# Row work, statistics and weight loads in other slots, and the spreads of the inverted denominators issued from ScalarE

## The chip, the cores and the metric

The kernel runs on one core of one Trainium2 chip. The metric is the device time of one execution in microseconds (us), as the median of several runs. All times below are microseconds unless marked otherwise. The engines are PE (TensorE, matmuls), DVE (VectorE), ACT (ScalarE), POOL (GpSimd) and SP (SyncE, which here only issues DMAs). Each engine works through a queue of its own in order, and waits on semaphores for the others.

## The reference

One transformer block in float32 over 16 sequences of 256 rows and 256 columns: self attention, cross attention to a context of 192 columns, and a gated feed-forward part (FFN).

```python
def _attention(xq, xkv, wq, wk, wv, wo, bo):
    q = (xq @ wq).reshape(B, S, N_HEADS, D_HEAD)
    k = (xkv @ wk).reshape(B, T, N_HEADS, D_HEAD)
    v = (xkv @ wv).reshape(B, T, N_HEADS, D_HEAD)
    attn = jnp.einsum('bihd,bjhd->bhij', q, k) * D_HEAD ** (-0.5)
    attn = jax.nn.softmax(attn, axis=-1)
    out = jnp.einsum('bhij,bjhd->bihd', attn, v).reshape(B, S, D_ATTN)
    return out @ wo + bo
h = _layernorm(x, ln1_g, ln1_b)
x = _attention(h, h, sa_wq, sa_wk, sa_wv, sa_wo, sa_bo) + x
h = _layernorm(x, ln2_g, ln2_b)
x = _attention(h, cond_emb, ca_wq, ca_wk, ca_wv, ca_wo, ca_bo) + x
h = _layernorm(x, ln3_g, ln3_b)
p = h @ ff_w1 + ff_b1
a, gate = (p[..., :D_FF], p[..., D_FF:])
h = a * jax.nn.gelu(gate, approximate=False) @ ff_w2 + ff_b2
return h + x
```

There are 16 heads of 64, so 8 pairs of heads, and D_FF is 1024.

## The kernel before

**Slots.** The work of the two attentions is cut into ATT = 256 slots, one for each pair of heads of each sequence, first all of self attention (slots 0 to 127), then all of cross attention (128 to 255). n counts the 32 pairs of a sequence and an attention; n from 16 on are the cross ones. Slot c is named by its scores. Each engine has a function that writes its part of slot c (pe_slot, act_slot, dve_slot, pool_slot, and on SP a loop in the block at L1549), and the order of the statements in it is the order in the engine's queue. Nothing is scheduled by a planner. After the slots comes the FFN: NCK = 8 chunks of two sequences, 8 steps each. gates(c) and second(c) are PE's two products of step c; the first steps are laced into the last slots by hand (L1849 on).

**One slot.** PE computes the scores S of slot c from RX (the split Q and K in a ring, brought there by SP's DMAs from QKS), projections QKB of a later pair, values VB, the output product WOP of an earlier slot, the transposes PTB of the exponentials of slot c-1, and the product with the values PVB of slot c-2. DVE takes the maximum of the scores (NM, L945), ACT the exponential with its sum (PT, DEN, L780). DVE inverts the sums (RDEN, L985) and turns them (RDT, L987). ACT copies the transposed exponentials to PH (L813), DVE makes their low part PL (L889). Both parts of QKB go to QKS: ACT's copy is the high part, DVE's split (L903) the low part. Every float32 matrix is multiplied as such a high and a low part.

**Denominators.** SP saves RDT to DRAM (save_den, L1605) and brings it back over 64 partitions for each of the two heads (spread_den, two DMAs into RB, L1616). ACT copies half of PVB into ON (L756), DVE adds the other half (L965), POOL multiplies ON by RB (L1143). Its count is pl_or.

**Row work.** The rows of a sequence are normalised some slots before it starts: start_of(n) = 8n - 20 from n = 6 on. Relative to that slot DVE takes the statistics at -4 (dve_stats), aggregates at -3, and POOL makes the reciprocal root at -3; DVE normalises at -1 (dve_normalize, L850) into the buffer near(n); SP stores the rows at 0, ACT loads them turned at +1 (L681), DVE turns them at +2, ACT applies gain and bias at +3 and +4 (L664), and POOL splits them after that. The context rows of cross attention are loaded by ACT at -5 to -3 (L699). Every fourth slot, c = 3 modulo 4, DVE adds four finished slots of WOP to the residual XR (L915, L919).

**Rows of the FFN.** chunk 0 and chunk 1 are prepared within the last slots. In dve_attention_slot their statistics (L831) and normalisations (L850) stand behind all of dve_slot, that is at the slot's end: chunk 0 at c = FFN_START - 16 to - 9 (FFN_START = ATT - 10 = 246), chunk 1's statistics at ATT - 6 to ATT - 4 and its normalisation in step 3 of the FFN. ACT rounds chunk 1 (L1325, L1330) in step 6, act_copy_raw (L1253) copies first products aside (RAW) while QKB is still shared with the attention.

## Time and profile before

| what | us |
|---|---|
| median of 3 runs (lowest to highest) | 1696.74 (1695.99 to 1697.89) |
| the profiled execution, whole | 1697.57 |
| its span, first to last instruction | 1695.8 |
| PE busy | 1680.5 (99%) |
| DVE busy | 1396.4 (82%) |
| ACT busy | 1247.5 (74%) |
| POOL busy | 1079.5 (64%) |

The profiled execution is 0.83 above the median of the runs. The granted clock of TensorE is 1.000 over the whole span. Busy time is arithmetic only: issuing a DMA occupies an engine's queue and is listed apart, as ACTq or SPq. In a timeline a line gives start and duration of a group of equal instructions (x4 is four of them), and in brackets the idle time ahead of the first and what ended it. A matmul's end is modelled: the next one of a pipelined row starts before it.

### The profile page before, as it was taken

The page shows a single profiled execution, that of the slowest core. Times are in us where ns is not written, and L with a number is a line of the kernel's source. Part 1 is how long each engine was busy: PE and PEld are TensorE (multiplying, and loading weights), DVE is VectorE, ACT ScalarE, POOL GpSimd, SP SyncE. Part 2 cuts the span into 40 slices and gives each one's busy share as a digit, 9 for nine tenths or more (in the row PEclk, how much of TensorE's full clock was granted, in tenths as well). Part 3 has the DMA queues.
Part 4 walks back from the last instruction along what each step waited for, and adds up shares of the span by engine and source line. Part 5 has one row for each costly group of instructions (what it writes and reads, how often), then busy time and mean ns, then how long its engine had stood idle before and what let it go on. Part 6 is the DMA issues. An engine that isn't in the chain of part 4 may idle for free.

```text
span 1695.8 us, 39063 instructions
## 1 busy us (share of the span) xinstructions
PE 1680.5 (99%) x11712; PEld 1560.7 (92%) x11712; DVE 1396.4 (82%) x2964; ACT 1247.5 (74%) x3379; POOL 1079.5 (64%) x1804
## 2 busy tenths in 40 slices
PE   8999999999999999999999999999999999999999
PEld 8999999999999999999999999999999998888888
DVE  8887888888888888889888888888888877656665
ACT  7788788888888888888888888888888886122221
POOL 7776577777766666787777777777777565231211
PEclk9999999999999999999999999999999999999999
DMA  7776677778766567887787878787776785212110
GB/s 214 183 180 161 171 208 190 204 198 211 196 176 159 153 167 200 230 222 185 190 209 196 205 196 210 193 210 182 197 177 176 192 211 139 69 50 72 64 40 26
DMA packets 301138, 288.91 MB, mean 170 GB/s; under 512 B 103425, under 2 KB 252033, under 8 KB 300929
## 3 DMA queue, kind: packets, MB, share of 16 engines
q1 hardware_dynamic: 247136, 273.29, 61.8%
q10 hardware_dynamic: 53792, 13.12, 3.5%
q8 instruction: 96, 1.57, 0.4%
q14 instruction: 114, 0.93, 0.2%
HBM read 82.98 MB, written 37.49 MB: 71 GB/s over the span
## 4 chain that ended last, share of the span: by engine, by line
PE 89%; DVE 3%; SPq 3%; issue 2%; POOL 1%; DMA 1%; ACT 1%; ACTq 0%; DVEq 0%; POOLq 0%
PE QKB L556 16%; PE PVB L638 13%; PE PTB L569 11%; PE WOP L620 10%; PE VB L491 8%; PE S L458 6%; PE S L459 6%; PE S L1282 5%; PE PTB L1282 5%; PE QKB L1304 3%; PE VB L1304 3%; PE QKB L538 2%; SPq L673 1%; SPq L675 1%; SPq L1616 1%
## 5 line engine op out<-in xcount | busy, mean ns | idle before, releaser
L780 ACT ACTIVATE PT<-S,NM 128x256 f32<-128x256 f32 x1024 | 471.9, 473 | 147.2 <-DVE NM L945 146.0
L889 DVE TENSOR_TENSOR PL<-PTB,PH 128x512 fp32r<-128x512 f32 x512 | 350.9, 686 | 128.2 <-ACT PH L813 127.9
L1143 POOL TENSOR_TENSOR ON<-ON,RB 128x256 f32<-128x256 f32 x256 | 188.1, 735 | 287.4 <-DVE ON L965 265.5
L945 DVE TENSOR_REDUCE NM<-S 128x2 f32<-128x512 f32 x512 | 327.3, 681 | 0.3
L813 ACT ACTIVATE PH<-PTB 128x1024 fp32r<-128x1024 f32 x256 | 264.3, 1032 | 67.9 <-PE PTB L569 66.3
L569 PE MATMUL PTB<-IDN,PT 128*128 128x128 f32 x2048 | 265.7, 273 | 0.1
L458 PE MATMUL S<-RX 128*128 128x256 f32 x1012 | 253.9, 283 | 0.8 <-DMA RX<-QKS 0.8
L459 PE MATMUL S<-RX 128*128 128x256 f32 x1012 | 253.7, 283 | 0.0
L556 PE MATMUL QKB<-HT,WQ 128*128 128x512 f32 x936 | 242.9, 394 | 0.9
L620 PEld LDWEIGHTS WOP<-WO,OT 128*128 128x128 f32 x1536 | 217.5, 190 | 20.1 <-POOL OT L1148 0.2
L569 PEld LDWEIGHTS PTB<-IDN,PT 128*128 128x128 f32 x2048 | 229.5, 140 | 1.1 <-issue 0.5
L620 PE MATMUL WOP<-WO,OT 128*128 128x256 f32 x1536 | 224.3, 282 | 0.0
L965 DVE TENSOR_TENSOR ON<-PVB,ON 64x256 f32<-64x256 f32 x512 | 213.4, 417 | 3.6
L756 ACT ACTIVATE ON<-PVB 64x256 f32<-64x256 f32 x512 | 194.2, 379 | 22.5 <-issue 5.0
L780 ACT ACTIVATION_READ_ACCUMULATOR PT<-S,NM 128x1 f32 x1024 | 207.7, 203 | 0.0
L1148 POOL TENSOR_TENSOR OT<-ON,OT 128x256 fp32r<-128x256 f32 x256 | 189.9, 742 | 20.5
L1124 POOL TENSOR_TENSOR VR<-VF,VR 128x256 fp32r<-128x256 f32 x256 | 189.1, 739 | 20.5
L458 PEld LDWEIGHTS S<-RX 128*128 128x128 f32 x1012 | 193.4, 191 | 1.2 <-DMA RX<-QKS 1.2
L459 PEld LDWEIGHTS S<-RX 128*128 128x128 f32 x1012 | 194.3, 192 | 0.0
L556 PEld LDWEIGHTS QKB<-HT,WQ 128*128 128x128 f32 x936 | 165.7, 189 | 30.4 <-DVE QKS L903 3.2
L638 PE MATMUL PVB<-PH,VR 128*128 128x256 f32 x1024 | 183.4, 300 | 0.7 <-issue 0.6
L638 PE MATMUL PVB<-PL,VR 128*128 128x256 f32 x1024 | 163.4, 282 | 0.0
(163 smaller groups left out, 2918.7 us busy)
## 6 DMA issues: line engine op xcount, KB each, us to landing
RX<-QKS SPq DMA_DIRECT2D x506, 192.0 KB, 2.9
RX<-QKS SPq DMA_DIRECT2D x506, 128.0 KB, 2.8
RB<-denominators SPq DMA_DIRECT2D x512, 64.0 KB, 2.7
out_dram<-XR SPq DMA_DIRECT2D x32, 256.0 KB, 3.5
weights_qk<-SPL SPq DMA_DIRECT2D x32, 256.0 KB, 3.4
WQ<-weights_qk SPq DMA_DIRECT2D x32, 256.0 KB, 3.4
rows<-XN SPq DMA_DIRECT2D x24, 256.0 KB, 2.6
rows<-HF SPq DMA_DIRECT2D x23, 256.0 KB, 2.7
```

The source lines that it names most:

```text
L458: e.matmul(o, q, RX[:, c % 2, i, K1, :], start=True, stop=False)
L459: last = e.matmul(o, q, RX[:, c % 2, i, K2, :], start=False, stop=True)
L556: last = e.matmul(QKB[:, :], w_pair(w, wp, p), act, start=i == 0, stop=i == len(passes) - 1)
L569: last = e.transpose(PTB[:, i, kt * S + qt * P:kt * S + (qt + 1) * P], PT[:, s % 2, q0:q0 + P], IDN[:, :])
L620: last = e.matmul(WOP[:, t * D:(t + 1) * D], OT[:, op, t * P:(t + 1) * P], WO[:, p, wp, :], start=begins(s) and t == 0 and j == 0, stop=en ...
L638: last = e.matmul(PVB[:, i * S:(i + 1) * S], VR[:, s // 2 % 2, kt, s % 2, i * P:(i + 1) * P], part[:, first:first + S], start=i == 0 and j ...
L756: last = e.activation(ON[OWN[i], s % 2, :], PVB[OTHER[i], i * S:(i + 1) * S], ACT.Copy)
L780: last = e.activation(PT[:, c % 2, j * S:(j + 1) * S], S1[:, i, qt * S:(qt + 1) * S], ACT.Exp, bias=NM[:, j:j + 1], accum_out=DEN[:, c % 2 ...
L813: e.activation(PH[:, s % 2, :], PTB[:, :, :].rearrange("p i n -> p (i n)"), ACT.Copy) \
L889: e.tensor_tensor(PL[:, cols], PTB[:, i, :], PH[:, s % 2, cols].bitcast(F32), ALU.subtract).then_inc(a.dve_pl, 1)
L945: e.tensor_reduce(NM[:, i * TT:(i + 1) * TT], S1[:, i, :].rearrange("p (t s) -> p t s", t=TT), AX.X, ALU.max, negate=True).then_inc(a.dve_ ...
L965: last = e.tensor_tensor(on, PVB[OWN[i], i * S:(i + 1) * S], on, ALU.add)
```

## The change

Lines of the changed kernel lie some 9 to 56 further on than the same lines before.

1. **normalized_in.** For n = 6 to 15 the normalisation moves from start_of(n) - 1 to start_of(n) - 2. The others stay.
2. **First value copies.** The copies VF of slots 0 to 7 wait for pl_v >= v - 3 instead of v.
3. **Spreads.** spread_den moves from SP to ACT's queue, behind the copies ON of the slot, with the same two waits.
4. **dve_ffn_rows.** The statistics and normalisations of FFN chunks 0 and 1 move into the slot, behind the other row work and ahead of the reciprocal. For chunk 1 the statistics go to ATT - 12 to - 10, the reciprocal root on POOL to ATT - 9, the normalisation to ATT - 7 to - 4, one tile per slot. SP stores those rows at ATT - 5 and - 3; act_copy_raw(4) and (5) wait for these stores, and the loads of these rows for their halves on DVE. In the FFN the turns of chunk 1 are made in steps 3 and 4 (5 and 6 before), and ACT rounds it in step 4 (6 before).
5. **Loads on SP.** The third and fourth quarters' chunks, load_four and the load of BOUT are issued in other slots.
6. **PE.** gates(5) goes before second(1).

```diff
@@ -154,6 +154,15 @@
+def normalized_in(c):
+    n = due(c, -2, 2)
+    if n and OLD // PAIRS + 2 <= n < B:
+        return n
+    n = due(c, -1, 2)
+    return None if n and OLD // PAIRS + 2 <= n < B else n
...
@@ -742,6 +751,18 @@
+        def spread_den(e, s):
+            e.wait_ge(d_ds[s % 4], 16 * (s // 4 + 1))
+            if s >= 2:
+                e.wait_ge(a.pl_or, s - 1)
+            else:
+                e.wait_ge(s_ow, s + 1)
+            for i in range(2):
+                e.dma_start(RB[OWN[i], s % 2, :],
+                            DS[s % 4, TT * i:TT * (i + 1), :].rearrange("t p -> (t p)").partition_broadcast(P // 2)) \
+                    .then_inc(d_rb[s % 2], 16)
...
@@ -755,6 +776,9 @@
                     last = e.activation(ON[OWN[i], s % 2, :], PVB[OTHER[i], i * S:(i + 1) * S], ACT.Copy)
                 last.then_inc(a.act_lp, 1)
+            if 0 <= c - 2 < ATT:
+                spread_den(e, c - 2)
             if due(c, 1, 2):
                 act_load_rows(e, due(c, 1), 0, 1)
...
@@ -925,14 +949,43 @@
-            if due(c, -1, 2):
-                e.wait_ge(a.dve_th, due(c, -1) - 1)
-                dve_normalize(e, sl, a, due(c, -1), (near(due(c, -1)),))
+            n = normalized_in(c)
+            if n:
+                e.wait_ge(a.dve_th, n - 1)
+                dve_normalize(e, sl, a, n, (near(n),))
...
+        def dve_ffn_rows(e, c):
...
+            if c == ATT - 12:
+                e.wait_ge(a.dve_xo, B + HOLD + 4)
+                dve_stats(e, zero_ffn, fs, 1, 0, 1)
+            if c == ATT - 11:
+                dve_stats(e, zero_ffn, fs, 1, 2, 3)
+            if c == ATT - 10:
+                dve_aggregate(e, zero_ffn, fs, 1)
+            if c == ATT - 7:
+                e.wait_ge(fs.s_ht, KD)
+            if ATT - 7 <= c < ATT - 3:
+                dve_normalize(e, zero_ffn, fs, 1, ROWS, (c - ATT + 7,))
...
@@ -968,7 +1021,7 @@
-                sl.wait(e, a.pl_v, v)
+                sl.wait(e, a.pl_v, v - 3)
...
             dve_rows(e, sl)
+            dve_ffn_rows(e, c)
...
@@ -1253,6 +1307,8 @@
             e.wait_ge(fs.pe_raw, n + 1)
+            if n in (4, 5):
+                e.wait_ge(d_fs[n - 4], 16 * 2)
...
@@ -1312,6 +1368,8 @@
                 e.wait_ge(d_fs[h], 16 * (chunk + 1))
+                if chunk == 1:
+                    e.wait_ge(fs.dve_hf, 2)
...
@@ -1352,7 +1410,7 @@
-            if c >= 0 and c % PAIRS == 6 and sl.has(c + PAIRS):
+            if c >= 0 and c % PAIRS == (6 if c >= PAIRS else 4) and sl.has(c + PAIRS):
...
@@ -1434,10 +1492,10 @@
-                if f == (2 if chunk else 3):
+                if f == 2 and chunk:
                     sl.wait(e, fs.s_ht, KD * (chunk + 1))
                     dve_normalize(e, sl, fs, chunk + 1, ROWS)
-                turn = f - (4 if chunk else 5)
+                turn = f - (4 if chunk else 3)
...
@@ -1684,12 +1709,14 @@
+                            turns = ((0, 1, 2, 3), (0, 1, 3, 4))[quarter - 2]
...
-                            if c == at + chunk:
+                            if c == at + turns[chunk]:
...
-                            if c == four + 2 + 2 * n:
+                            if c == four + 2 + (n if g == 0 else 3 * n):
...
@@ -1745,19 +1772,19 @@
-                if c == ATT - PAIRS:
+                if c == ATT - 19:
                     e.wait_ge(a.pl_xb, 2 * B)
                     e.dma_start(BOUT[:, :], ff_b2.partition_broadcast(P)).then_inc(d_bo, 16)
             for c in range(-AHEAD, ATT + 2):
-                if c >= 2:
-                    spread_den(c - 2)
...
+                if c in (ATT - 5, ATT - 3):
+                    store_ffn_rows(1, (c - ATT + 5) // 2)
...
@@ -1862,8 +1890,8 @@
             pe_outputs(e, ATT - 3)
+            pe_gates(e, EARLY + 1)
             pe_second(e, 1)
-            pe_gates(e, EARLY + 1)
             pe_outputs(e, ATT - 2)
```

DVE in slots 66 and 67 of self attention, before the change, from the sum of slot 66's two ON halves (L965) to the turn of slot 67's denominators. L903 is the split, L919 the residual sum, L850 the normalisation of n = 11.

```order
L965 TENSOR_TENSOR ON<-PVB,ON 64x256 x2
L985 RECIPROCAL RDEN<-DEN 128x4
L987 STREAM_TRANSPOSE RDT<-RDEN 128x32
L903 TENSOR_TENSOR QKS<-QKB,QKS 128x2x256
L889 TENSOR_TENSOR PL<-PTB,PH 128x512
L945 TENSOR_REDUCE NM<-S 128x2 x2
L889 TENSOR_TENSOR PL<-PTB,PH 128x512
L965 TENSOR_TENSOR ON<-PVB,ON 64x256 x2
L919 TENSOR_TENSOR XR<-WOP,XR 128x512
L850 TENSOR_SCALAR XN<-XR,MV,RSTD 128x2x4x32 x2
L985 RECIPROCAL RDEN<-DEN 128x4
L987 STREAM_TRANSPOSE RDT<-RDEN 128x32
```

The same stretch after the change.

```order
L1018 TENSOR_TENSOR ON<-PVB,ON 64x256 x2
L874 TENSOR_SCALAR XN<-XR,MV,RSTD 128x2x4x32 x2
L1039 RECIPROCAL RDEN<-DEN 128x4
L1041 STREAM_TRANSPOSE RDT<-RDEN 128x32
L927 TENSOR_TENSOR QKS<-QKB,QKS 128x2x256
L913 TENSOR_TENSOR PL<-PTB,PH 128x512
L998 TENSOR_REDUCE NM<-S 128x2 x2
L913 TENSOR_TENSOR PL<-PTB,PH 128x512
L1018 TENSOR_TENSOR ON<-PVB,ON 64x256 x2
L943 TENSOR_TENSOR XR<-WOP,XR 128x512
L1039 RECIPROCAL RDEN<-DEN 128x4
L1041 STREAM_TRANSPOSE RDT<-RDEN 128x32
```

The two normalisations have gone from slot 67, which has the residual sum, to slot 66, ahead of the reciprocal and the split there.

ACT in slot 144 of cross attention before, from the copies ON to the exponentials. L664 is a gain and bias, L699 a load of context rows.

```order
L756 ACTIVATE ON<-PVB 64x256 [waits pl_o,pe_pv]
L756 ACTIVATE ON<-PVB 64x256
L664 ACTIVATE HF<-HF,LNG 128x256 [waits dve_th]
L699 DMA XN<-in_ctx_dram 32x8x32 [waits dve_th]
L780 ACTIVATE PT,DEN<-S,NM 128x256 [waits dve_nm,dve_rc,pe_t]
L780 ACTIVATE PT,DEN<-S,NM 128x256
L780 ACTIVATE PT,DEN<-S,NM 128x256 [waits dve_nm]
L780 ACTIVATE PT,DEN<-S,NM 128x256
```

The same place after the change.

```order
L777 ACTIVATE ON<-PVB 64x256 [waits pl_o,pe_pv]
L777 ACTIVATE ON<-PVB 64x256
L762 DMA RB<-denominators 64x256 [waits pl_or,d_ds2]
L762 DMA RB<-denominators 64x256
L673 ACTIVATE HF<-HF,LNG 128x256 [waits dve_th]
L708 DMA XN<-in_ctx_dram 32x8x32 [waits dve_th]
L804 ACTIVATE PT,DEN<-S,NM 128x256 [waits dve_nm,dve_rc,pe_t]
L804 ACTIVATE PT,DEN<-S,NM 128x256
L804 ACTIVATE PT,DEN<-S,NM 128x256 [waits dve_nm]
L804 ACTIVATE PT,DEN<-S,NM 128x256
```

The two DMAs into RB now stand behind the copies ON and ahead of the gain and bias and the four exponentials, and they wait for a multiplication on POOL (pl_or) and for the save of the denominators (d_ds2).

PE at the entry of the FFN before, from the output product of slot ATT - 3. L1304 is the second product, L1282 the gates.

```order
L620 MATMUL WOP<-WO,OT 128x256 x6
L1304 MATMUL QKB<-WV,QKS 128x256 x6
L1304 MATMUL VB<-WV,QKS 128x256 x6
L1282 MATMUL PTB<-HT,WQ 128x512 x12
L620 MATMUL WOP<-WO,OT 128x256 x6
L1304 MATMUL QKB<-WV,QKS 128x256 x6
L1304 MATMUL VB<-WV,QKS 128x256 x6
L620 MATMUL WOP<-WO,OT 128x256 x6
```

The same place after the change.

```order
L629 MATMUL WOP<-WO,OT 128x256 x6
L1338 MATMUL PTB<-HT,WQ 128x512 x12
L1360 MATMUL QKB<-WV,QKS 128x256 x6
L1360 MATMUL VB<-WV,QKS 128x256 x6
L629 MATMUL WOP<-WO,OT 128x256 x6
L1360 MATMUL QKB<-WV,QKS 128x256 x6
L1360 MATMUL VB<-WV,QKS 128x256 x6
L629 MATMUL WOP<-WO,OT 128x256 x6
```

The twelve matmuls of gates(5) now stand ahead of the second product of step 1; everything around is as before.

## Rows read from the trace of the kernel before

**Rows 1.** Page, part 1: engine, busy us, share of the span, instructions.
```profile
PE 1680.5 (99%) x11712; PEld 1560.7 (92%) x11712; DVE 1396.4 (82%) x2964; ACT 1247.5 (74%) x3379; POOL 1079.5 (64%) x1804
```
**Rows 2.** Waits of PE's weight loads: waiter, releaser: us in all, count, longest.
```profile
PEld QKB L556 <- DVE QKS L903: 3.2, 11, 0.3
...
PEld PVB L638 <- issue: 2.3, 8, 0.4
```
**Rows 3.** Timeline (start, us, engine, line, operation), PE in three slots of self attention.
```profile
395.33 0.28 PE L458 MATMUL S<-RX 128*128 128x256 f32 x1
...
396.29 1.55 PE L556 MATMUL QKB<-HT,WQ 128*128 128x512 f32 x6
...
400.89 0.28 PE L458 MATMUL S<-RX 128*128 128x256 f32 x1
...
406.80 0.28 PE L458 MATMUL S<-RX 128*128 128x256 f32 x1
```
**Rows 4.** Timeline, DVE in the same slots.
```profile
393.94 0.69 DVE L903 TENSOR_TENSOR QKS<-QKB,QKS 128x512 fp32r<-128x512 f32 x1
...
395.64 0.69 DVE L889 TENSOR_TENSOR PL<-PTB,PH 128x512 fp32r<-128x512 f32 x1 [1.01 <-ACT PH L813]
...
399.87 1.25 DVE L850 TENSOR_SCALAR XN<-XR,MV,RSTD 128x256 f32<-128x256 f32 x2
...
401.38 0.65 DVE L903 TENSOR_TENSOR QKS<-QKB,QKS 128x512 fp32r<-128x512 f32 x1
```
**Rows 5.** Timeline, DVE near the start.
```profile
18.33 0.42 DVE L972 COPY VF<-VB 128x256 f32<-128x256 f32 x1 [0.69 <-POOL VR L1124]
```
**Rows 6.** Timeline, PE: first scores of two slots of cross attention, twelve slots apart.
```profile
1285.72 0.28 PE L458 MATMUL S<-RX 128*128 128x256 f32 x1
...
1351.55 0.28 PE L458 MATMUL S<-RX 128*128 128x256 f32 x1
```
**Rows 7.** Timeline, SP and PE before slot 251.
```profile
1391.02 0.62 SPq L675 DMA_DIRECT2D RX<-QKS  x1
...
1392.61 1.10 SPq L1616 DMA_DIRECT2D RB<-denominators  x2
...
1396.07 0.39 PE L458 MATMUL S<-RX 128*128 128x256 f32 x1 [0.79 <-DMA RX<-QKS]
```
**Rows 8.** Timeline, ACT and its DMA issues (ACTq), self and cross attention.
```profile
501.34 1.94 ACTq L681 DMA_DIRECT2D HF<-rows  x2
...
811.32 0.77 ACT L756 ACTIVATE ON<-PVB 64x256 f32<-64x256 f32 x2
...
812.73 0.48 ACT L780 ACTIVATE PT<-S,NM 128x256 f32<-128x256 f32 x1 [0.65 <-DVE NM L945]
...
816.55 0.32 ACTq L699 DMA_DIRECT2D XN<-in_ctx_dram  x1
...
816.65 0.77 ACT L756 ACTIVATE ON<-PVB 64x256 f32<-64x256 f32 x2
```
**Rows 9.** Timeline, ACT, DVE and PE around a slot with gain and bias.
```profile
822.94 0.60 ACT L664 ACTIVATE HF<-HF,LNG 128x256 f32<-128x256 f32 x1
...
829.73 0.85 DVE L965 TENSOR_TENSOR ON<-PVB,ON 64x256 f32<-64x256 f32 x2
...
831.32 0.72 PE L638 MATMUL PVB<-PH,VR 128*128 128x256 f32 x4
```
**Rows 10.** Timeline, PE and ACT at the entry of the FFN.
```profile
1433.94 0.98 PE L1304 MATMUL QKB<-WV,QKS 128*128 128x256 f32 x6 [0.60 <-DVE QKS L1418]
...
1443.05 1.20 PE L1282 MATMUL S<-HT,WQ 128*128 128x512 f32 x4 [1.57 <-DVE PT L1412]
...
1451.98 0.81 ACT L1325 ACTIVATE PH<-XN,LNG 128x512 fp32r<-128x512 f32 x1 [5.19 <-DVE HF L1364]
...
1454.81 0.67 ACT L1353 ACTIVATE PT<-PTB,B 128x512 f32<-128x512 f32 x1
...
1456.37 1.88 PE L1282 MATMUL S<-PH,WQ 128*128 128x512 f32 x7 [1.82 <-POOL PH L1383]
```

More of the change, by code:

```diff
@@ L935, in dve_rows @@
                 dve_aggregate(e, sl, a, due(c, -3))
+        def dve_ffn_rows(e, c):
+            if c == FFN_START - 16:
+                e.wait_ge(a.dve_xo, B + HOLD + 2)
+                dve_stats(e, zero_ffn, fs, 0, 0, 1)
+            if c == FFN_START - 15:
+                dve_stats(e, zero_ffn, fs, 0, 2, 3)
+            if c == FFN_START - 14:
+                dve_aggregate(e, zero_ffn, fs, 0)
+            if c == FFN_START - 12:
+                e.wait_ge(a.s_ht, 4 * B)
+                e.wait_ge(a.pl_ct, 2 * B)
+            if FFN_START - 12 <= c < FFN_START - 8:
+                dve_normalize(e, zero_ffn, fs, 0, ROWS, (c - FFN_START + 12,))
+            if FFN_START - 6 <= c < FFN_START - 4:
+                dve_ffn_turn(e, 0, c - FFN_START + 6)
+            if c == ATT - 12:
[9 more added lines that the diff above has]
+                dve_normalize(e, zero_ffn, fs, 1, ROWS, (c - ATT + 7,))
         def dve_slot(e, sl):
@@ L1496, in dve_attention_slot @@
                 dve_aggregate(e, sl, a, 1)
-            if c == FFN_START - 16:
-                e.wait_ge(a.dve_xo, B + HOLD + 2)
-                dve_stats(e, zero_ffn, fs, 0, 0, 1)
-            if c == FFN_START - 15:
-                dve_stats(e, zero_ffn, fs, 0, 2, 3)
-            if c == FFN_START - 14:
-                dve_aggregate(e, zero_ffn, fs, 0)
-            if c == ATT - 6:
-                e.wait_ge(a.dve_xo, B + HOLD + 4)
-                dve_stats(e, zero_ffn, fs, 1, 0, 1)
-            if c == ATT - 5:
-                dve_stats(e, zero_ffn, fs, 1, 2, 3)
-            if c == ATT - 4:
-                dve_aggregate(e, zero_ffn, fs, 1)
-            if c == FFN_START - 12:
-                e.wait_ge(a.s_ht, 4 * B)
-                e.wait_ge(a.pl_ct, 2 * B)
-            if FFN_START - 12 <= c < FFN_START - 8:
-                dve_normalize(e, zero_ffn, fs, 0, ROWS, (c - FFN_START + 12,))
-            if FFN_START - 6 <= c < FFN_START - 4:
-                dve_ffn_turn(e, 0, c - FFN_START + 6)
         def pool_low(e, *ns):
@@ L1538, in pool_attention_slot @@
                 pool_ffn_low(e, 1)
-            if sl.c == ATT - 3:
+            if sl.c == ATT - 9:
+                e.wait_ge(fs.dve_xn, 2)
                 pool_rstd(e, zero_ffn, fs, 1)
@@ L1606, in save_den @@
                             RDT[:, s % 2, :]).then_inc(d_ds[s % 4], 16)
-            def spread_den(s):
-                e.wait_ge(d_ds[s % 4], 16 * (s // 4 + 1))
-                if s >= 2:
-                    e.wait_ge(a.pl_or, s - 1)
-                else:
-                    e.wait_ge(s_ow, s + 1)
-                for i in range(2):
-                    e.dma_start(RB[OWN[i], s % 2, :],
-                                DS[s % 4, TT * i:TT * (i + 1), :].rearrange("t p -> (t p)").partition_broadcast(P // 2)) \
-                        .then_inc(d_rb[s % 2], 16)
             def stage_cross(n):
@@ L1690, in fill_weights @@
                             at = j - LEAD + 2
+                            turns = (0, 1, 2, 3)
                         for chunk in range(4):
-                            if c == at + chunk:
+                            if c == at + turns[chunk]:
                                 if chunk == 0:
@@ L1774, in _ @@
                 if chunk + 1 < NCK:
-                    store_ffn_rows(chunk + 1, 0, 1)
+                    if chunk:
+                        store_ffn_rows(chunk + 1, 0, 1)
                     load_ffn_rows(e, chunk + 1, *range(8))
```

## The prediction

> **What bounds the kernel now.** I read the engine totals first [rows 1]: PE is busy 1680.5 of 1695.8 us, 99%. No edit here removes a matmul, so all that can be won is what PE still waits, and all that can be lost is a new wait. The list of PE's waits comes next [rows 2]: the largest kind is the weight load of the joint projections (QKB) on the split of Q and K on DVE, 3.2 us in 11 waits, and the first product with V (PVB) waits 2.3 us in 8 places for its semaphores. The timeline then tells what the list hides. A matmul row is drawn 0.28 long, but the next one starts 0.12 later, so a wait under about 0.16 shows as no idle time; starts of slots have to be set against each other. The slots of self attention start at 395.33, 400.89 and 406.80 [rows 3]: 5.56, then 5.91. The reader is to see that one slot in eight is 0.35 too long, without an idle mark. The clock was at its full level in every slice, so I leave it out.
>
> **Part A, the normalisation of sequences 7 to 15.** In the slot of 5.91 DVE does two normalisations at 399.87 (1.25) right before the split at 401.38, behind which QKB starts [rows 3, 4]; in that same slot stands the residual sum of 0.7. The change takes the 1.25 out of it and puts it a slot earlier. There the split ended at 393.94 + 0.69 = 394.63, and QKB started at 396.29 [rows 3, 4]: 1.66 of slack against 1.25, so 0.41 is left; and the next DVE operation, PL at 395.64, had been idle 1.01, so it starts at most 0.24 later, which PV two thirds of a slot on does not feel. The wait goes, and nothing is late next. This holds for n = 7 to 15, nine slots: 9 x 0.35 = **3.2**. Sequences from 16 on are not moved, since the range ends at the 16 of self attention. If only half of the moved work fitted, it would be 1.6.
>
> **Part B, the first value copies.** DVE's copy VF at 18.33 had stood idle 0.69 behind the multiplication VR on POOL [rows 5]. Waiting for a product three slots older ends that; next in line would be PE's product VB itself. I take **0.6**, between 0 (something else of the start comes last) and 0.7.
>
> **Part C, row work in front of the split and earlier.** From the scores at 1285.72 to those at 1351.55 lie 12 slots of cross attention [rows 6]: 65.83, against 12 x 5.33 = 63.96, 1.9 over. (5.33 is the distance of ON copies in a quiet place, 811.32 to 816.65 [rows 8].) In these slots DVE does the statistics, normalisation and turns of the first FFN rows at the slot's end, behind the split, where they delay the maximum (NM) of the next scores. The same operations now stand ahead of the reciprocals. Where a slot holds 5.9 of DVE work for 5.33, which happens in two, no order helps. I take 1.4. Likewise the last twelve slots hold the second chunk's statistics at the slot's end; three of the eight PVB waits lie there [rows 2]. These statistics go to ATT-12 to -10, its normalisation to ATT-7 to -4, one tile each. I take 0.8. Together **2.2**, between 1.0 and 2.7. New is that the raw copies 4 and 5 on ACT wait for the stores of these rows. Those are issued at ATT-5 and -3, the copies stand at ATT-3 and -2. Even with the 5.05 from issue to use of the RX in [rows 7] a store lands within one slot, so the second is just in time. Behind a waiting raw copy stand the copy PH and so PV. I price it at nothing, at most 1.
>
> **Part D, the spreads leave SyncE.** Each slot two DMAs bring the inverted denominators back over 64 partitions each. On SP the pair takes 1.10 [rows 7]. Late in the attentions SP is full: RX is issued at 1391.02, and the scores that read it start at 1396.07 after 0.79 idle (0.96 by starts) [rows 7]. Without 1.1 per slot ahead of it, and with one load of weights gone to a slot eleven earlier, RX is issued about that much sooner. I count 1.0 here and 0.3 for a smaller wait of the same kind five slots before: **1.3**, between 0 and 1.6. What speaks against it: of the 5.05 from issue to use most is the transfer, which an earlier place in a queue doesn't shorten. The Trainium skill ("DMA: Bandwidth & Descriptors", section "Issuing engines are not separate DMA queues") says that starting DMAs from several engines saves only the sequencer's time to start them, usually small next to the DMA. Here the rows bear it out in part: the time to start a pair, 1.10, is a fifth of the 5.05, and by the strict rule part D would be 0 and the sum 1.3 less.
>
> **What the spreads cost on ACT.** The trace shows no such pair on ACT. Nearest rows [rows 8]: single issues on ACT of 0.32 (twice 0.64, the low end), the SP pair of 1.10 [rows 7], and a pair on ACT of 1.94 (the high end, at 501.34). I take 1.10, since it is the same transfer with the same descriptors. ACT's queue starts an issue before the arithmetic ahead of it has ended: 816.55 against 816.65 for the copy ON [rows 8]. So the pair lies from -0.1 to 1.0 behind the first ON copy, whose two parts end at 0.77, while Exp starts at 812.73 - 811.32 = 1.41, idle 0.65 on NM [rows 8]. Up to 1.45 a pair costs nothing. Its own two waits: the save of the denominators, one slot old and landed, and the multiplication on POOL of two slots back, which is done where ON's own wait is. Queued behind the pair are Exp, PH and with them PE. The cover is missing where ACT has the gain and bias (L664, 0.60) in the same gap [rows 9]: Exp is then later by about 0.5, PH and DVE's ON (829.73 + 0.85 = 830.58, against PV at 831.32, 0.74 of slack [rows 9]) with it, 0.2 is left. Some 26 slots of cross attention are such; long issues will eat the 0.2 in some. I take 0.7 for them and 0.8 for single long issues over the 253 other slots: **-1.5**, between 0 and -5.
>
> **Part E, the entry of the FFN.** PE waits 0.60 at 1433.94 for the split QKS, 1.57 before gates 6 at 1443.05 and 1.82 before gates 8 at 1456.37 [rows 10]; by starts 0.76, 1.7 and 1.98. Gates 5 now go before the second product: they need nothing of it, so the 0.76 is filled. Gates 6 still wait for DVE behind the last sum: -0. Gates 8 waited for Gelu at 1454.81, which stood on ACT behind gain and rounding of chunk 1 from 1451.98, 2.83, which had waited 5.19 for its turn [rows 10]. The change does this one step earlier. From gates 6 (T0), the turn ends about T0 + 2.05, the rounding T0 + 4.9, Gelu and the multiplication behind it (1454.81 to 1456.37, 1.56) T0 + 6.45. PE needs (1456.37 - 1443.05 - 1.98) / 2 = 5.67 for a step [rows 10]. So gates 7 wait 0.8, and gates 8 no more. Gain 0.76 + 1.98 - 0.8 = 1.9, **2.0** with a gap of 0.1 that closes beside it; between 0.8 (rounding later by its loads) and 2.7.
>
> Turns of weight loads on SP move by a slot or two and have a slot of room on either side; with the stores, 0.
>
> **The sum.** 3.2 + 0.6 + 2.2 + 1.3 + 2.0 - 1.5 = 7.8. The profiled execution took 1697.57, so it would take 1689.8. It lies 0.83 above the median of the runs, so the median would be **1689.0**.
>
> **Rivals.**
> 1. ACT pays. The spreads land their issue time on Exp in gain slots and beside loads: 26 slots x 0.15 = 3.9 and two or three of 0.5 make 5.0 of the 1.5, and 9.3 - 5.0 = 4.3: 1697.57 - 4.3 - 0.83, about **1692.4** (1691.5 to 1694.5). For: the slack of 0.2 in rows 9; against: Exp idles 0.65 in most slots.
> 2. The gains are not there: something else came last in A and C (the copies on ACT, which now carry the issues), or the raw copies wait for their stores. About **1696.5**.
> 3. Slower. Exp, PH, PV and the scores of the next slot form a loop through ACT with 5.33 per slot. If an average pair on ACT takes over about 1.5, Exp is late in every slot and nothing is left over to catch up. With 1.94, the high end [rows 8], over two slots' slack of 0.9 each slot loses about 0.27: 253 x 0.27 = 68, less 8: about **1756**. It decides at 1.5 to 1.7. For: a pair of 1.94 exists. Against: that was a pair of larger transfers, and SP's take 1.10.
>
> **How the numbers follow.** Forecast 0.70 (own range 1686.5 to 1691.5), rival 1 0.17, rival 2 0.05, rival 3 0.08. The low end takes costs at 0.7 and gains near their tops: 1685.5. The high end takes in rival 1, 1694.5. 0.2% of 1696.7 is 3.4 us, about what a measurement can tell from no change; rival 1 lies half within it. Faster 0.70 + 0.08 = 0.78, same 0.09 + 0.05 = 0.14, slower 0.08.
>
> **What the profile after would show.** A: slots from n = 7 on of 5.56 instead of 5.91, and the QKB waits on QKS nearly gone. B: no idle before the VF copies. C: the 12 slots under 64.6. D: no scores wait for RX, SP's queue with gaps; on ACT pairs near 1.1 and idle before Exp still there in most slots, less than 0.65. E: the first product without a wait, a wait of 0.8 before gates 7, none before gates 8. Wrong would be: pairs on ACT over 1.5, Exp without idle time in front of it, PV waiting for PH, or slots of cross attention over 5.33 on average.

## The result, and the profile after

The changed kernel takes 1701.42 us (1699.89 to 1703.87, 15 runs), the kernel before beside it 1697.76 (1695.89 to 1698.98, 15 runs). The ratio is 1.0025, with a 95% interval of 1.0017 to 1.0033: slower by 0.25%, 4.2 us (the medians differ by 3.7). Forecast were 1689.0 and a range from 1685.5 to 1694.5. The profiled execution has a span of 1700.1 against 1695.8.

The first view is the page of the changed kernel: the engine totals, the chain of work that ended last, by engine, and a line of the DMA issues (what, from which queue, count, size, us from issue to landing).

```profile
PE 1687.0 (99%) x11712; PEld 1564.0 (92%) x11712; DVE 1399.8 (82%) x2964; ACT 1235.4 (73%) x3379; POOL 1079.6 (64%) x1804
...
PE 84%; ACT 6%; DVE 4%; issue 3%; ACTq 2%; DMA 1%; POOL 0%; SPq 0%; DVEq 0%; POOLq 0%
...
RB<-denominators ACTq DMA_DIRECT2D x512, 64.0 KB, 2.8
```

PE still reads as 99% busy, as in [rows 1]. The chain tells more: ACT with its DMA issues now holds 8% of it, and in the kernel before ACT and ACTq together held 1%. ACT's own busy time went down by 12 us (1247.5 to 1235.4) while ACT became what PE waits for: issues are not counted as busy.

Where the time went is best seen by cutting both spans at the first scores of the same slots. The windows view gives length, PE, PEld, DVE, ACT and POOL busy with counts, PE's clock, DMA share and GB/s. Of the kernel before, slots 121 to 231, 231 to 243 and 243 to 255:

```profile
698.04:1285.72 587.68, 587.39 (x4184) 550.27 (x4183) 524.45 (x1127) 500.73 (x1402) 452.85 (x779) 1.00 0.79 199
1285.72:1351.55 65.83, 65.44 (x469) 60.72 (x468) 57.71 (x128) 53.04 (x153) 39.76 (x68) 1.00 0.68 178
1351.55:1417.46 65.91, 64.92 (x489) 61.48 (x488) 51.16 (x114) 54.31 (x152) 40.52 (x67) 1.00 0.81 207
```

The same slots of the changed kernel:

```profile
694.12:1294.36 600.24, 596.00 (x4184) 552.07 (x4183) 526.13 (x1130) 495.61 (x1404) 452.18 (x779) 1.00 0.76 194
1294.36:1358.78 64.42, 64.42 (x470) 60.68 (x468) 58.47 (x128) 54.40 (x153) 40.84 (x69) 1.00 0.73 194
1358.78:1422.73 63.95, 63.95 (x489) 61.37 (x488) 53.61 (x117) 53.88 (x152) 39.99 (x66) 1.00 0.78 216
```

With the same 4184 matmuls the long middle stretch, which is nearly all of cross attention, costs 600.24 instead of 587.68: 12.6 lost. The two stretches behind it gain 1.4 and 2.0. Slot 121 itself starts 3.9 earlier (694.12 against 698.04), which is the gain of the start and of self attention. From slot 255 to the end 1.0 is gained. The sum: -3.9 + 12.6 - 3.4 - 1.0 = +4.3, the difference of the spans.

One sequence of the middle stretch, timeline of ACT from the copy PH of slot 151 to the first exponential of slot 153, in the changed kernel (start, us, operation; ACTq is an issue; in brackets the idle time ahead and what ended it):

```profile
862.14 1.03 ACT L837 ACTIVATE PH<-PTB 128x1024 fp32r<-128x1024 f32 x1
862.14 1.22 ACTq L708 DMA_DIRECT2D HF<-in_ctx_dram  x2
863.46 0.38 ACT L777 ACTIVATE ON<-PVB 64x256 f32<-64x256 f32 x1 [0.29 <-issue]
863.58 0.45 ACTq L762 DMA_DIRECT2D RB<-denominators  x1
863.86 0.38 ACT L777 ACTIVATE ON<-PVB 64x256 f32<-64x256 f32 x1
864.06 1.50 ACTq L762 DMA_DIRECT2D RB<-denominators  x1
865.62 0.60 ACT L673 ACTIVATE XN<-XN,LNG 128x256 f32<-128x256 f32 x1 [1.38 <-issue]
865.64 0.99 ACTq L708 DMA_DIRECT2D HF<-in_ctx_dram  x1
866.75 0.47 ACT L804 ACTIVATE PT<-S,NM 128x256 f32<-128x256 f32 x1 [0.53 <-issue]
...
872.01 0.47 ACT L804 ACTIVATE PT<-S,NM 128x256 f32<-128x256 f32 x1 [0.64 <-DVE NM L998]
```

And PE's first scores of slots 152, 153 and 154 there:

```profile
862.88 0.28 PE L467 MATMUL S<-RX 128*128 128x256 f32 x1
...
868.82 0.35 PE L467 MATMUL S<-RX 128*128 128x256 f32 x1 [0.44 <-ACT PT L804]
...
874.97 0.28 PE L467 MATMUL S<-RX 128*128 128x256 f32 x1
```

The reader is to see three things. An issue runs beside the arithmetic instruction that is under way (L708 starts with PH at 862.14), but what stands behind it in the queue waits for it: ON starts 0.1 after the two issues end. From the first copy ON at 863.46 to the first exponential at 866.75 it is 3.29, and it was 1.41 in [rows 8]. And the scores of the next slot wait for these exponentials: the slots take 5.94 and 6.15 instead of 5.33. This one sequence loses 1.4 in two slots, and the waits named "ACT PT" are only the visible part; the rest shows in PE's weight loads as "issue":

```profile
PE S L467 <- ACT PT L804: 1.9, 4, 0.6
...
PEld PVB L647 <- issue: 4.8, 15, 0.4
PEld S L467 <- issue: 2.8, 5, 0.8
PEld QKB L565 <- DVE QKS L927: 2.4, 8, 0.4
```

Against [rows 2] the waits for the split went from 11 to 8 only, as new ones came in cross attention, and those of PVB doubled.

Sorted by their place among the eight slots of a sequence, 9.9 of the 12.6 lie in the three slots of each eight that stand with or right behind the loads of context rows (136 to 138, 144 to 146 and so on). Nearly all of the other 2.7 lie in slots 132, 140, 164, 180, 196, 212 and 228, of 5.68 to 5.79, where ACT has no such load. There ACT waits for DVE, which does a residual sum and two normalisations and has no idle time to catch up in. ACT in slot 212:

```profile
1192.98 0.48 ACT L804 ACTIVATE PT<-S,NM 128x256 f32<-128x256 f32 x1 [1.38 <-DVE NM L998]
```

In the kernel before these slots take 5.33 (one 5.37), and in e13 below, where the context loads are left out, all 5.33. So they are late only because the slots ahead of them were.

### The profile page after: what moved, and what is told of

It is laid out like the page before. It is cut to its first block, busy times and chain, and to the rows that moved or that the text cites. A ratio compares the mean times of both kernels' runs of the same rounds, so it can differ in the third digit from the quotient of the medians.

```text
span 1700.1 us, 39063 instructions
## 1 busy us (share of the span) xinstructions
PE 1687.0 (99%) x11712; PEld 1564.0 (92%) x11712; DVE 1399.8 (82%) x2964; ACT 1235.4 (73%) x3379; POOL 1079.6 (64%) x1804
## 3 DMA queue, kind: packets, MB, share of 16 engines
q8 instruction: 96, 1.57, 0.4%
## 4 chain that ended last, share of the span: by engine, by line
PE 84%; ACT 6%; DVE 4%; issue 3%; ACTq 2%; DMA 1%; POOL 0%; SPq 0%; DVEq 0%; POOLq 0%
PE QKB L565 14%; PE PVB L647 12%; PE PTB L578 11%; PE WOP L629 9%; PE VB L500 8%; PE S L467 6%; PE S L468 6%; PE S L1338 5%; PE PTB L1338 5%; ACT PT L804 3%; PE QKB L547 3%; PE QKB L1360 3%; PE VB L1360 3%; ACT PH L837 2%; DVE NM L998 1%
```

## The experiments

Theory: the spreads' issue time, put into ACT's queue where loads of context rows are issued too, makes the queue of three slots in eight longer than the slots. Rivals: the moved row work or weight loads cost the time; every pair on ACT costs something wherever it stands; its position ahead of the exponentials is what hurts.

**e1: spreads back on SP, all else as changed.**

```diff
-            if 0 <= c - 2 < ATT:
-                spread_den(e, c - 2)
...
             for c in range(-AHEAD, ATT + 2):
+                if c >= 2:
+                    spread_den(e, c - 2)
```

> The changed kernel with the spreads back in SyncE's queue, at the same place in it as before; everything else as changed. In the two traces the changed kernel lost 12.6 us between the slots 121 and 231 (cross attention) and gained 0.8 at the start, 3.1 in self attention, 3.4 from slot 231 to 255 and 0.9 at the entry of the FFN, 8.2 together. Theory (issue time on ACT ahead of the exponentials): the 12.6 go, the gains stay but for at most 1.0 of the wait for RX: 1689.5 to 1690.5, against about 1697.8 of before. Rival (the moved row work or the moved weight loads cost the 12.6): it stays at 1700 to 1702.

Measured: 1689.34 (1688.87 to 1689.51), ratio to before 0.9954 (0.9940 to 0.9968). The whole loss is gone, and what is left of the change is worth 8. From slot 121 to 231 it takes what the kernel before took: first scores at 693.82 and 1281.38, 587.56.

**e2: the kernel before with the spreads on ACT and nothing else** (the calls as in the change's diff).

> The kernel before with part 3 of the change alone: the spreads in ACT's queue behind the copies ON. Theory: the loss of 12.6 without the gains, less up to 1.0 for a shorter wait for RX: 1709 to 1710.5. Rival (moved row work costs it): 1697 to 1698.

Measured: 1710.47 (1709.61 to 1711.06), ratio 1.0079 (1.0065 to 1.0093). So the spreads alone cost 13, and the rest of the change neither causes nor cures it.

**e3: the loads of context rows moved behind PH.** Is it the place ahead of the exponentials?

```diff
-            for k in range(3):
-                if due(c, k - 5, B):
-                    act_load_ctx(e, due(c, k - 5, B), *((0,), (3,), (6, 7))[k])
...
-            for k in range(2):
+            for k in range(3):
                 if due(c, k - 5, B):
-                    act_load_ctx(e, due(c, k - 5, B), *((1, 2), (4, 5))[k])
+                    act_load_ctx(e, due(c, k - 5, B), *((0, 1, 2), (3, 4, 5), (6, 7))[k])
```

> The changed kernel with the loads of context rows that stand in ACT's queue ahead of the exponentials (one or two of a slot, in three slots of eight) moved behind the copy PH, where the others of them stand already; the spreads stay on ACT. Theory (it is the sum of a pair of 1.1 and loads of 0.6 to 1.6 in a gap of 1.4 that delays the exponentials): nearly all of the 12.6 goes, at most 3 stay for the gain and bias and the loads of rows: 1690 to 1692.5. Rival (the pair alone is too long, or waits for its semaphores): 1700 to 1702.

Measured: 1708.05 (1706.17 to 1709.24), ratio 1.0063 (1.0051 to 1.0076). The expectation was wrong by some 16 us, and it was even worse than the change itself. ACT's timeline of slot 135 to 136 in it:

```profile
781.64 1.04 ACT L834 ACTIVATE PH<-PTB 128x1024 fp32r<-128x1024 f32 x1
781.64 2.65 ACTq L708 DMA_DIRECT2D HF<-in_ctx_dram  x3
784.39 0.38 ACT L777 ACTIVATE ON<-PVB 64x256 f32<-64x256 f32 x1 [1.72 <-issue]
```

Three issues behind PH take 2.65, of which PH covers 1.04. The copy ON, and the pair behind it, are late by what the exponentials were spared. So it isn't the place in the slot: the gap of 1.41 that the prediction costed is not a private reserve, it is what one queue has left over in a slot.

That e3 is slower than the change itself is another matter. 5.5 of it is one slot, 131, of 10.79. DVE waits there for context rows that ACT issued at 743.44 to 744.28 (DVE):

```profile
752.46 0.71 DVE L896 STREAM_TRANSPOSE HF<-XN 128x512 f32<-128x512 f32 x1 [4.57 <-DMA XN<-in_ctx_dram]
```

Without this slot's excess e3 takes 599.1 from slot 121 to 231 and the changed kernel 600.2: moving the loads within the queue changed next to nothing.

**e4: spreads on SP only in slots with such loads.**

```diff
+def loads_in(c):
+    return c - 2 >= 2 and bool(due(c, 1, 2) or any(due(c, k - 5, B) for k in range(3)))
...
-            if 0 <= c - 2 < ATT:
+            if 0 <= c - 2 < ATT and not loads_in(c):
```

> The changed kernel with the spreads on SP in just those slots where ACT has loads of rows or of context rows ahead of the exponentials, and on ACT in all others (about seven of ten). Theory: pairs in slots without loads cost nothing, so 1689 to 1690.5. Rival (every pair on ACT costs its share): about 0.7 of 12.6 stays, 1698 to 1699.

Measured: 1692.40 (one of the 8 runs was far off, at 5906.76; without it the median is the same within 0.01), ratio 0.9971 (0.9960 to 0.9981). Taking 156 of 512 spreads off ACT brought back 9 of the 12; the rival's 1698 is ruled out. But 3 us against e1 stay, 3.6 between slots 121 and 231 in the profile. 1.4 of it are slots 131 and 132, and 1.5 are slots 159, 175 and 223. ACT in slot 131, then in slot 157 to 158:

```profile
751.37 1.16 ACTq L767 DMA_DIRECT2D RB<-denominators  x2
752.65 0.48 ACT L809 ACTIVATE PT<-S,NM 128x256 f32<-128x256 f32 x1 [3.24 <-issue]
```
```profile
893.58 2.15 ACTq L695 DMA_DIRECT2D XN<-rows  x2
```

The first pair is issued 2.73 after the copy ON at 748.64: it waits for the save of the denominators, which SP had issued at 744.80 behind a weight load, and the exponentials wait with it. In the second the two loads of turned rows took 2.15 in place of the 1.00 in the changed kernel, and the copies ON and the pair behind them came late; slots 175 and 223 have such a pair of loads of 2.11 and 2.21 ahead of them. So a pair in a slot without context loads is free only while its own waits and its neighbours' issues are short.

**e5 and e6: one DMA over 128 partitions in place of two over 64,** on SP and on ACT.

```diff
-            for i in range(2):
-                e.dma_start(RB[OWN[i], s % 2, :],
-                            DS[s % 4, TT * i:TT * (i + 1), :].rearrange("t p -> (t p)").partition_broadcast(P // 2)) \
-                    .then_inc(d_rb[s % 2], 16)
+            e.dma_start(RB[:, s % 2, :],
+                        DS[s % 4, 0:2 * TT, :].rearrange("(h t) p -> h (t p)", h=2).unsqueeze(1)
+                        .broadcast_to((2, P // 2, S))).then_inc(d_rb[s % 2], 16)
```

> The kernel of e1 (changed, spreads on SP), with one DMA over 128 partitions per slot in place of the two over 64. Theory: SP's queue is not what bounds it except at the one wait for RX (1.1 us near slot 251 in e1): 1688 to 1689.5. Were SP's queue the limit in more places, 1687 or less. If issue time goes by the rows described and not by the instruction, nothing changes: 1689.3.

> The changed kernel (spreads on ACT) with one DMA per slot in place of two. Theory: in the three slots of eight with loads of context rows ACT's queue (arithmetic and issues together) was taken 14.8 of 16.0 us before the change, so 1.2 were free, and three pairs of 1.1 don't fit. One issue of 0.6 needs 1.8 less what overlaps with arithmetic: the loss of 12.6 falls to 2 to 5, 1691 to 1694.5. If issue time goes by the rows and one DMA of 128 partitions takes the 1.1 of the pair: 1701.

Measured: 2034.88 (ratio 1.1976, 1.1953 to 1.1999) and 1868.53 (1.1006, 1.0989 to 1.1023). Neither says anything on the queue, because the transfer became slow. In e5 (timeline of SP, then of POOL, one slot):

```profile
1003.13 0.57 SPq L761 DMA_DIRECT2D RB<-denominators  x1
...
1011.13 0.73 POOL L1193 TENSOR_TENSOR ON<-ON,RB 128x256 f32<-128x256 f32 x1 [3.99 <-DMA RB<-denominators]
```

The issue does cost half of the pair, 0.57. But its data are awaited until 1011.13, 8.0 after the issue, where a spread of the pair lands after 2.7 by the page. The Trainium skill says why ("DMA: Bandwidth & Descriptors", section "Rules for kernel authors"): the slowest dimension of the access pattern sets how many DMA engines take part, and a leading dimension of 2 leaves at most two. The trace agrees: for each of the 256 DMAs of e5 the awaited semaphore rises at three moments, a first at 1.0 us and two more, the last at 6.2 (medians), while for each of the pairs' DMAs in e1 it rises 16 times.

**e9: the loads of context rows on SP instead of ACT.**

```diff
+                for k in range(3):
+                    if due(c, k - 5, B):
+                        act_load_ctx(e, due(c, k - 5, B), *((0, 1, 2), (3, 4, 5), (6, 7))[k])
                 weights(c)
                 fill_weights(c)
```

> The changed kernel (spreads on ACT) with all loads of context rows moved from ACT's queue to SP's; the loads of turned rows stay on ACT. Theory (what counts is the sum of arithmetic and issues in ACT's queue over the slots with these loads, not where in the slot an issue stands): the loads that leave take about as much as the pairs add there, so of the 12.6 lost in cross attention at most 2 stay: 1689 to 1691. Rival (the spreads themselves are badly placed ahead of the exponentials, with whatever is beside them): 1697 or more.

Measured: 1699.71 (1696.65 to 1702.66), ratio 1.0016 (1.0007 to 1.0025). By the time alone this is the rival. The trace splits it in two. From slot 137 to slot 169 it loses 0.3 against the kernel before, where the changed kernel loses 3.9: in these sequences all but one slot take 5.33. All DMAs of the changed kernel are still there, so it is ACT's queue that lost the time there, and not their traffic. The loss of e9 sits in single places, and SP's fuller queue makes both kinds of them. Slots 170 and 171 have one of each (ACT, then DVE, then PE):

```profile
962.42 1.15 ACTq L762 DMA_DIRECT2D RB<-denominators  x2
963.70 0.47 ACT L801 ACTIVATE PT<-S,NM 128x256 f32<-128x256 f32 x1 [1.93 <-DVE NM L992]
...
967.06 0.71 DVE L893 STREAM_TRANSPOSE XN<-HF 128x512 f32<-128x512 f32 x1 [2.79 <-DMA HF<-in_ctx_dram]
...
968.85 0.50 PE L565 MATMUL QKB<-CT,WQ 128*128 128x512 f32 x1 [1.30 <-DVE QKS L921]
```

The copies ON there started at 961.01; the pair starts 1.41 after them, since it waits for the save of the denominators, which SP issued only at 958.34, behind context loads and a weight load (SP):

```profile
955.52 2.05 SPq L708 DMA_DIRECT2D HF<-in_ctx_dram  x3
957.62 0.62 SPq L1607 DMA_DIRECT2D STG<-in_L_xattn_ff_w_dram  x1
958.34 0.57 SPq L1636 DMA_DIRECT2D denominators<-RDT  x1
```

The other semaphore of the pair, POOL's multiplication at 959.22, had long come. This costs 0.31: slot 170 takes 5.64. The 1.67 of slot 171 (7.00) is the other kind: DVE waits 2.79 for context rows that SP issued last at 962.22, and its split, and with it PE's QKB, come late. Slots 186 to 188 lose 1.8 in all behind another pair, 1.45 late, whose two issues then take 1.97, and slots 121 to 134, with two late pairs more, lose 2.6 more than in the kernel before; how much of that the pairs cost stays open. Eight pairs of cross attention are issued over 0.2 after the copy ON began in e9, none in the changed kernel. The wait that the spread carries into ACT's queue is thus a second, separate price, which is paid where SP saves the denominators late, here and in slot 131 of e4.

**e13: no loads of context rows at all** (the calls on ACT and DVE's wait for them removed).

```diff
-                    act_load_ctx(e, due(c, k - 5, B), *((0,), (3,), (6, 7))[k])
...
-                    act_load_ctx(e, due(c, k - 5, B), *((1, 2), (4, 5))[k])
...
-            e.wait_ge(d_cx, 128 * (n - B + 1))
```

> The changed kernel (spreads on ACT) with the 128 loads of context rows left out, and DVE's wait for them: the cross attentions then work on stale rows, so it leaves part of the loading out, while every arithmetic instruction stays. Theory (the sum in ACT's queue): pairs, gain and bias and arithmetic fit into every slot, so the slots of cross attention take 5.33 and at most 2 of the 12.6 stay: 1689 to 1690.5. Rival (the pairs cost something in every slot, or wait for their semaphores): 1694 or more.

Measured: 1690.60 (1690.50 to 1691.48), ratio 0.9959 (0.9946 to 0.9971). Slots 121 to 231 in its windows view:

```profile
695.14:1283.50 588.36, 587.90 (x4184) 550.35 (x4183) 523.28 (x1127) 495.54 (x1402) 452.11 (x779) 1.00 0.72 192
```

588.36, where the changed kernel takes 600.24 and the kernel before 587.68. All 512 spreads are on ACT here, with both of their waits, and 0.7 of the 12.6 is left. This settles it: the pair fits into every slot, gain and bias slots too, if no context loads are beside it. Long pairs of 1.5 to 2.0 do too: from slot 148 to 222 e13 has eight, and no slot there takes over 5.37. Only one of 2.35, in slot 133, goes with slots of 5.94 and 5.66. Counted from the traces, ACT's queue (arithmetic and issues, overlap counted once, from the copy ON in the slot ahead of the first context load, over three slots, mean of 12 sequences) was taken 14.8 us in the kernel before. Three slots of 5.33 are 16.0. In the changed kernel it is 16.1, in e3 16.4; in e13, e9 and e4 it is 15.4, and what e9 and e4 lose stands mostly in the single places shown above.

**e10: the normalisation alone,** on the kernel before.

> The kernel before with part A alone, the normalisation of the sequences 7 to 15 one slot earlier. Theory: nine slots of 5.91 become 5.56, 3.2 less than before. Rival (the gain in the trace came from another part that was changed with it): no difference.

Measured: 1693.33 (1692.16 to 1696.95), ratio 0.9979 (0.9970 to 0.9987). That is 3.7 less, and the 3.2 lies within its interval.

**e15 and e16: which edit shortens the last slots?** e15 is e1 with the row work of chunk 0 back at the slot's end; e16 is the kernel before with only this edit:

```diff
-                if c == ATT - PAIRS:
+                if c == ATT - 19:
                     e.wait_ge(a.pl_xb, 2 * B)
```

> The kernel of e1 with the row work of FFN chunk 0 (statistics, normalisation, turn) back at the end of the slots 230 to 241. Theory (part C as predicted): 1.4 more than e1, 1690.8, with slots of 5.5 to 5.9 between 231 and 243. Rival (the long slots 240 to 242 of the kernel before were chance of its one profile, as e10 shortened them without this edit): 0.3 to 0.5 more than e1, 1689.7.

> The kernel before with the load of BOUT at ATT-19 instead of ATT-8 and nothing else. Theory (this load in front of RX made the wait at slot 251): the slot before 251 takes 5.33 and not 6.29, 1.0 less than before, 1696.2. Rival (e11, which put it back, kept the slot at 5.33: the wait needs SP otherwise full, or comes by chance): no difference.

Measured: e15 1690.88 (1690.49 to 1690.93), 1.5 more than e1, as part C had it; by the ratios to the kernel before beside each (0.9958 and 0.9954) it is only 0.7, and the spans differ by 1.3. But the long slots 240 to 242 do not come back in it: of the kernel before's excess there, some was of its one profile. e16 1696.08, ratio 0.9989 (0.9980 to 0.9998): 1.9 less (by the interval 0.3 to 3.4), with slot 250 at 5.33 instead of 6.29. In e2 and e10, which have the load where the kernel before has it, this slot takes 6.08 and 6.53. So the wait for RX in [rows 7] hung on this load. **e11** puts the load back in a kernel with all other edits:

> The kernel of e7 (spreads on SP) with only the load of BOUT back at ATT-8 from ATT-19. The slot before 251 took 6.29 in the kernel before and 5.33 in e1, e7 and the changed kernel alike, wherever the spreads were issued. Theory (this load ahead of RX on SP made that wait, not the spreads): 1.0 more than e7, 1687.6, with the slot at 6.3. Rival (the weight loads moved beside it): the same as e7.

Measured: 1688.44 against 1686.59 of e7, 1.9 more, but with the slot at 5.33 in its profile. The profiled execution is the fastest of the five, 1686.85, and the others take 1688.41 to 1688.73, so it can have missed the wait. Both tests give 1.9 where 1.0 was expected, and the intervals of e7 and e11 overlap. Where the time is paid when SP is otherwise as in the change stays open.

**e7, e8, e12, e14: the rest of the entry of the FFN.** e7 is e1 with DVE's last residual sum one step later:

```diff
             dve_ffn(e, Slot(3, FU, 2))
+            dve_ffn(e, Slot(4, FU, 2))
             dve_slot(e, Slot(ATT + 3, ATT))
             e.wait_ge(a.dve_xo, 2 * B)
-            ffn(e, dve_ffn, 4)
+            ffn(e, dve_ffn, 5)
```

> The kernel of e1 with DVE's last residual sum of the attentions behind step 4 of the FFN's DVE work instead of ahead of it. PE waits 1.6 for the product of gates 4 (gates 6 need its bank) that stands behind this sum, which itself waits for the last output product. Theory: the 1.6 and a wait of 0.3 after it go, 1687 to 1688. Rival (gates 6 or 7 then wait for the rounding of chunk 1 or for Gelu): 1689.

> The kernel of e7 with the spreads on ACT from slot 242 on only, where ACT has no loads of rows any more. Between slots 243 and 255 the changed kernel gained 1.96, e1 only 0.67, with a wait of 1.1 for RX. Theory (part D of the prediction is real): 1.0 to 1.3 less than e7. Rival (the raw copies on ACT make up for it): the same as e7.

> The kernel of e7 with ACT's gain and rounding of chunk 1 in step 5 of the FFN instead of 4, so behind the Gelu of step 5. PE waits 0.76 for gates 7, whose bank is freed only by the product behind that Gelu (the wait that the prediction priced at 0.8). Theory: it goes, 0.7 less than e7, 1685.9. Rival (gates 8 then wait for the rounded rows): the same as e7 or more.

> e8 (spreads on ACT from slot 242 on only, last residual sum later) with the rounding in step 5 of e12. e7, e8 and e12 measured the same, 1686.6 to 1686.8, yet in the profile of e12 the wait of 0.76 before gates 7 is gone and a wait of 0.74 for RX near slot 254 stands in its place, which e8 doesn't have. Theory (the two gains are real but small): 0.7 to 1.2 less than e7, 1685.4 to 1686. Rival (something behind them sets the time): 1686.6.

Measured: e7 1686.59 (1685.85 to 1687.66), ratio 0.9937 (0.9925 to 0.9949). PE at gates 6 in e1, then PE at gates 6 and 7 in e7:

```profile
1436.24 3.02 PE L1335 MATMUL S<-HT,WQ 128*128 128x512 f32 x12 [1.57 <-DVE PT L1467]
```
```profile
1433.16 2.91 PE L1335 MATMUL S<-HT,WQ 128*128 128x512 f32 x12
...
1439.54 1.67 PE L1335 MATMUL PTB<-HT,WQ 128*128 128x512 f32 x6 [0.60 <-DVE PT L1467]
```

The 1.57 goes, and the wait before gates 7 that the prediction priced at 0.8 is there, 0.76 by starts. e8 (1686.66) is no different from e7: the spreads on ACT late in the program bring nothing there. e12 (rounding in step 5) is at 1686.84 the same as well, although the 0.76 is gone from its profile; a wait of 0.74 for RX near slot 254 stands there. e14, all of these together, takes 1685.44 (1685.06 to 1686.05), ratio 0.9928 (0.9915 to 0.9940). That is the lowest median of all, 12.5 us under the kernel before beside it; its interval overlaps that of e7.

## Why the prediction was wrong

**The step that failed is "What the spreads cost on ACT": 1.5 was said, 12.6 it is.** Its pieces stood right: a pair on ACT takes 1.10 (median 1.105 in the trace after), an issue runs beside the copy ON, and a pair alone costs next to nothing (e13). The failure is what was laid beside it. It weighed the pair against a gap of 1.41 and asked what else is in that gap, and of the two things named in the order of slot 144 it took the gain and bias of 0.60 and left the context load out. Besides, it treated the gap as closed: the second pair of context loads behind PH, and the gain and bias, take from the same queue. The unit to count in was the queue over a slot, or over the three slots in a row with such loads, where 14.8 of 16.0 us were taken, and where the pairs, less what they overlap with, bring 1.3. e13 shows it from the one side, e3 from the other.

**Rival 1 was the right mechanism with the wrong size.** It had ACT paying in gain slots and beside loads, but at 26 x 0.15. In groups of eight slots from slot 133 on, cross attention loses between 0.4 and 1.8 each, 12.6 in all from slot 121 to 231, where the rival said 5 altogether. Rival 3, every slot late because a pair takes over 1.5, did not happen: in slots without loads the exponentials still wait 0.64 for NM.

**Part A** said 3.2. The slots of [rows 3] in the changed kernel (PE):

```profile
393.04 0.28 PE L467 MATMUL S<-RX 128*128 128x256 f32 x1
...
398.60 0.28 PE L467 MATMUL S<-RX 128*128 128x256 f32 x1
...
404.16 0.28 PE L467 MATMUL S<-RX 128*128 128x256 f32 x1
```

Both take 5.56 now. From slot 30 to 104 3.1 are won in the trace, and e10 measures 3.7.

**Part B** said 0.6: slot 5 starts 1.0 earlier than in the kernel before, in e1 as well. But it starts 0.2 to 0.65 earlier in e2, e10 and e16 too, which don't have this edit. The twelve profiles with it have slot 5 at 38.5 to 39.3 (without e5 and e6), the four without at 39.2 to 39.9. The means are 0.7 apart, which fits the 0.6, but the ranges overlap a little.

**Part C** said 2.2 with a bound of 1.0 to 2.7: slots 231 to 243 take 64.42 instead of 65.83, and slot 253 lost its 0.65. e15 gives 0.7 to 1.5 for chunk 0 alone. Yet 1.0 of the 1.4 in slots 231 to 243 also shows in the profiles of e10 and e16, which lack the edit. The 0.65 of slot 253 is the edit's: it shows in e1 and not in e10 and e16. The size of 2.2 is about right; where all of it is won isn't settled. The waiting raw copies cost nothing visible.

**Part D** said 1.3 for the spreads leaving SP. The wait that it named went by another edit: the wait at slot 251 goes in e1 and e16 as well, where the spreads are on SP, and stays in e2, where they are on ACT (slot 250 takes 6.08). But with the other edits in and the spreads on SP a new wait for RX stands four slots behind the one of [rows 7], before slot 255. PE in e1:

```profile
1410.77 0.39 PE L467 MATMUL S<-RX 128*128 128x256 f32 x1 [1.12 <-DMA RX<-QKS]
```

Slot 254 takes 6.17 in e1 and 6.15 in e15, 5.62 in e12, 5.12 in e7 and 5.00 in e11; in every profile of the changed kernel with the late spreads on ACT (e3, e4, e8, e9, e13 and e14 too) it takes 4.88. So leaving SP does save time late in the attentions, between 0.1 and 1.3 in one profile each, and the medians of e7 and e8 are too close to show it.

**Part E** said 2.0, and 1.0 came. PE at the entry, changed kernel:

```profile
1445.37 0.98 PE L629 MATMUL WOP<-WO,OT 128*128 128x256 f32 x6 [0.45 <-POOL OT L1202]
1447.92 4.54 PE L1338 MATMUL S<-HT,WQ 128*128 128x512 f32 x12 [1.57 <-DVE PT L1470]
```

The waits of 0.60 and 1.82 of [rows 10] are gone as said. New is 0.45 for the last OT on POOL: PE now gets there earlier than POOL does, a "what is late next" that was not asked. And gates 6 take 4.54 instead of 2.91, see below; e1, without that, gains 1.5 from slot 255 to the end.

All together, the gains were forecast at 9.3, or 8.0 without part D, and e1, which is the change without its third part, gains 7.9 (1697.19 to 1689.34). That the sum is so close is in part luck: 1.0 to 1.9 of it is the load of BOUT, which had no term of its own, part E came short, and e1 pays 1.3 before slot 255. The low end of the range has a slip, too: the tops of parts A to E add up to 10.9, less 0.7 for the spreads 10.2, which is 1686.5 and not 1685.5. Nothing hangs on it.

## What to carry to other kernels

A DMA that is moved to a compute engine's queue takes that engine's issue time, about 0.55 each here, less only what the one arithmetic instruction under way covers, and everything behind it waits, wherever in the loop body it stands. Whether the kernel pays depends on what room the queue has: between slots 121 and 231 the pairs cost 12.6 beside the context loads and 0.7 without them. Count the whole queue of that engine, arithmetic and issues, over the fullest iterations, since "busy" leaves the issues out. And when a transfer is merged to save an issue, look at the transfer again first: here it went from 2.7 to 8.0.

## What the runs showed of the hardware

The half clock came and went by itself. In the changed kernel's windows view (length, busy times, clock) around gates 6:

```profile
1444.00:1448.00 4.00, 1.98 (x15) 1.57 (x13) 2.48 (x6) 0.00 (x0) 3.92 (x6) 0.97 0.02 4
1448.00:1452.30 4.30, 4.30 (x13) 3.41 (x14) 1.72 (x4) 2.51 (x4) 0.91 (x2) 0.63 0.00 0
1452.30:1456.30 4.00, 4.00 (x30) 3.82 (x29) 2.90 (x4) 1.57 (x3) 3.89 (x5) 1.00 0.00 0
```

The granted clock falls from 2.4 GHz to 1.2 for most of 4.3 us, after 4 us in which PE was busy 1.98, and costs 1.6. The kernel before had PE busy 1.63 of 3.20 us at the same place and kept 1.00; e1 kept it with the same wait of 1.57. In the profiles of e4, e9 and e10 it fell at the entry of the FFN too. What decides it these traces don't show. Of the 15 runs of the changed kernel four have a mean clock of 0.999; their median is 1702.33, that of the others 1701.28, less apart than the runs among themselves (1699.89 to 1703.87).

An issue on the same queue has two prices. Most take 0.3 to 0.6, but 24 of the 512 spreads on ACT took over 1 us, up to 1.77; on SP in the kernel before it were 18 of 512. On ACT the exponentials feel them where the queue has no room: such an issue of 1.50 starts the slots of 5.94 and 6.15 shown above, while the eight long pairs of e13 lengthened no slot.
